# One attention kernel: the cross value sums of a half on eight blocks of TensorE at once, in one slot

## The reference, cut to what matters

```
q, k, v   = heads(xn @ Wq + bq), heads(xn @ Wk + bk), heads(xn @ Wv + bv)
y         = softmax(mask(q k^T) * scale) @ v                  # self
qc,kc,vc  = heads(xn @ Wcq + bcq), heads(ctx @ Wck + bck), heads(ctx @ Wcv + bcv)
y         = y + softmax(qc kc^T * scale) @ vc                 # cross: 64 keys
x         = x + tanh(g_xattn) * (y @ Wp + bp)
x         = x + tanh(g_ffn) * ffn(layernorm(x))
```

## Time and profile before

| | |
|---|---|
| median of three runs | 1546.71 us |
| the profiled execution | 1540.59 us, its span 1538.5 us, 2.1 us lie around it |
| TensorE (PE) busy | 1426.7 us, 93% of the span |
| VectorE (DVE), ScalarE (ACT), GpSimd (POOL) busy | 74%, 58%, 59% |
| mean granted TensorE clock | 0.989 of full speed |
| attention phase | about 21 to 1122 us: 16 batches, whole ones 67.9 us each |

### The profile page before, as it was taken

One profiled execution on the slowest core, in us unless ns is written; L12 is line 12 of the kernel. 1 busy time (PEld: TensorE's weight loads), 2 busy tenths in 40 slices (PEclk: granted clock), 3 DMA queues, 4 the chain that ended last, 5 costly groups with the idle time before them and its releaser, 6 DMA issues.

```text
span 1538.5 us, 36199 instructions
## 1 busy us (share of the span) xinstructions
PE 1426.7 (93%) x11288; PEld 948.6 (62%) x11288; DVE 1145.7 (74%) x3026; ACT 896.0 (58%) x1907; POOL 901.9 (59%) x1643
## 2 busy tenths in 40 slices
PE   4899999999999999999999999999979989898997
PEld 3556556655566566555655665665546778787675
DVE  6777887878778887878788787878644555565686
ACT  3466676666667676666667666665723555565210
POOL 4245566664756666575756657475654555665782
PEclk8899999999999999999999999999999999999999
DMA  6745454545454554645464454545555565454794
GB/s 169 198 131 138 140 151 141 172 135 165 135 160 146 157 169 120 183 133 151 134 177 144 136 180 126 159 134 172 178 152 160 169 221 170 150 153 143 230 351 165
DMA packets 184123, 250.01 MB, mean 162 GB/s; under 512 B 32024, under 2 KB 134560, under 8 KB 183936
## 3 DMA queue, kind: packets, MB, share of 16 engines
q1 hardware_dynamic: 149680, 185.60, 42.0%
q0 software_dynamic: 13008, 36.65, 6.6%
q10 hardware_dynamic: 21248, 25.46, 5.0%
HBM read 150.06 MB, written 95.97 MB: 160 GB/s over the span
## 4 chain that ended last, share of the span: by engine, by line
PE 63%; DVE 18%; ACT 11%; issue 5%; DMA 2%; POOL 1%; SPq 0%; DVEq 0%; ACTq 0%; POOLq 0%
PE vector_bank L2025 8%; PE pv_self L1529 8%; DVE nmax L1288 7%; PE scalar_bank L1465 7%; PE vector_bank L1502 5%; PE vector_bank L1575 4%; PE vector_bank L1439 3%; PE vector_bank L1499 3%; ACT q L857 3%; PE scalar_bank L1452 2%; PE scalar_bank L1455 2%; PE scalar_bank L1453 2%; ACT parts L866 2%; PE scalar_bank L2012 2%; ACT parts L873 2%
## 5 line engine op out<-in xcount | busy, mean ns | idle before, releaser
L1288 DVE TENSOR_REDUCE nmax<-vector_bank 128x1 f32<-128x384 f32 (+4 forms) x832 | 511.2, 639 | 74.4 <-PE vector_bank L1502 70.0
L929 ACT ACTIVATE pt<-scalar_bank 128x512 f32<-128x512 f32 x640 | 362.7, 605 | 175.6 <-PE scalar_bank L1465 167.1
L746 POOL TENSOR_SCALAR_AFFINE_SELECT pt<-pt 128x256 f32<-128x256 f32 (+1 forms) x640 | 222.7, 362 | 206.4 <-ACT pt L929 184.4
L1465 PE MATMUL scalar_bank<-stack 99*64 99x512 bf16 (+4 forms) x1280 | 284.2, 319 | 2.3 <-ACT pt L929 1.0
L1502 PE MATMUL vector_bank<-stack 96*128 96x128 bf16 (+3 forms) x1024 | 244.0, 301 | 0.0
L1854 POOL DMA_INDIRECT rows<-pt x143 | 139.1, 973 | 117.3 <-DVE pt L1983 63.2
L1499 PE MATMUL vector_bank<-tri,ident_b 128*128 128x128 bf16 (+2 forms) x704 | 175.3, 249 | 21.5 <-DMA stack<-qk_scratch 10.5
L1529 PE MATMUL pv_self<-pt,vst 128*32 128x512 f32 (+3 forms) x2048 | 161.1, 438 | 0.1
L705 POOL DMA_INDIRECT rows<-xn,slot x128 | 132.8, 1037 | 44.2 <-issue 26.3
L1499 PEld LDWEIGHTS vector_bank<-tri,ident_b 128*128 128x128 bf16 x704 | 67.0, 97 | 145.2 <-DVE nmax L1288 59.9
L2025 PE MATMUL vector_bank<-pt 128*128 128x128 f32 x1144 | 151.2, 275 | 0.1
(11 more groups left out here) (320 smaller groups left out, 2858.9 us busy)
## 6 DMA issues: line engine op xcount, KB each, us to landing
qk_scratch<-parts SPq DMA_DIRECT2D x31, 1200.0 KB, 4.5
stack<-qk_scratch SPq DMA_DIRECT2D x120, 192.0 KB, 3.0
pt<-rows SPq DMA_DIRECT2D x143, 132.0 KB
stack<-qk_scratch SPq DMA_DIRECT2D x248, 72.0 KB, 2.5
stack<-qk_scratch SPq DMA_DIRECT2D x124, 128.0 KB, 3.0
stack<-qk_scratch SPq DMA_DIRECT2D x240, 36.0 KB, 2.1
pt<-rows SPq DMA_DIRECT2D x8, 1024.0 KB, 8.7
stack<-rows SPq DMA_DIRECT2D x8, 1024.0 KB, 11.5
```

The source lines that it names most:

```text
L746: pool.affine_select(out=v, in_=v, compare_op=ALU.is_ge, fill=0.0, base=0, pattern=pat, channel_multiplier=-1).then_inc(masked, 1)
L929: act.activation(dst, bank(kind, b, ("st", c, k))[:, :], ACT.Exp, scale=SCALE).then_inc(scalar_drained, 1)
L1288: dve.tensor_reduce(dst, src, axis=AX, op=ALU.max, negate=True).then_inc(vector_drained, 1)
L1465: return pe.matmul(out, stack[c][0:rows, head, key0:key0 + nk], stack[c][0:rows, head, q0:q0 + nq], start=True, stop=True, **kw)
```

## The change

- Cross sums: all eight heads of a half in one place, slot 14, once the exponentials of X0 and X1 of the second group are done. Each head is a block of its own: 64 rows (its 64 keys), 32 columns, 512 moving columns. The four even heads (rows 0 to 63) write `pv_cross`, the four odd heads (rows 64 to 127) write `pv_self`. `vcst` loses its zero blocks.
- ScalarE copies both behind the exponential of slot 15, and s(c, 0) behind that of slot 22.
- The first self sums, which now wait for both of these copies, go from slots 16 and 20 to 17 and 21.
- The transposes of x go to slots (0, 19), (0, 23), (1, 18) and (1, 21); `yT`, `wp`, the statistics, `mT` and `xT` go to later slots.
- `recip` has a buffer for each sum, `yc` is one buffer in which x of the even and the odd heads interleave, and `normalise` of x waits for GpSimd's last addition from it.

```diff
-PREV_UNITS = {(0, 1): ("yT", 0), (0, 2): ("yT", 1), (0, 4): ("wp", 0), (0, 5): ("wp", 1), (0, 6): ("wp", 2), (0, 7): ("wp", 3),
+PREV_UNITS = {(0, 3): ("yT", 0), (0, 4): ("yT", 1), (0, 6): ("wp", 0), (0, 7): ("wp", 1), (0, 8): ("wp", 2), (0, 9): ("wp", 3),
-ROUTE_STEPS = {(0, 5): ("stats", 0), ..., (0, 10): "aggregate", (0, 14): "normalise", (0, 23): "max", ...
+ROUTE_STEPS = {(0, 7): ("stats", 0), ..., (0, 11): "aggregate", (0, 15): "normalise", (0, 23): "max", ...
-CUR_UNITS = {(1, 6): ("tU", 0, 1, "x"), (1, 11): ("tU", 0, 1, "s"),
-             (0, 2): ("mT", 0, 1), (0, 16): ("mT", 1, 0), (1, 2): ("mT", 1, 1)}
-NEXT_UNITS = {..., (1, 13): ("xT", 0), (1, 15): ("xT", 1), (1, 16): ("mT", 0, 0)}
+CUR_UNITS = {(1, 11): ("tU", 0, 1, "s"), (0, 19): ("tU", 0, 0, "x"), (0, 23): ("tU", 0, 1, "x"),
+             (1, 18): ("tU", 1, 0, "x"), (1, 21): ("tU", 1, 1, "x"),
+             (0, 5): ("mT", 0, 1), (0, 21): ("mT", 1, 0), (1, 4): ("mT", 1, 1)}
+NEXT_UNITS = {..., (1, 14): ("xT", 0), (1, 16): ("xT", 1), (1, 20): ("mT", 0, 0)}
...
-    PV = Events(of_current([(w, c, g) for c in range(KC) for g in range(2) for w in ("x", "s")]), LB, credit=8)
+    PV = Events(of_current([(w, c, g) for c in range(KC) for w in ("x", "s") for g in range(2)]), LB, credit=8)
...
-                act.activation(usum[w, g][:, :], (pv_cross if w == "x" else pv_self)[:, :], ACT.Copy).then_inc(pv_drained, 1)
+                act.activation(usum[w, g][:, :], (pv_cross if (w, g) == ("x", 0) else pv_self)[:, :], ACT.Copy).then_inc(pv_drained, 1)
...
-                        if c == 1 and k == 3:
-                            unnormalised(kind, b, "x", 0, 1)
                         if c == 1 and k == 8:
                             unnormalised(kind, b, "s", 0, 1)
-                        if k == 18:
-                            unnormalised(kind, b, "x", c, 0)
+                        if k == 15:
+                            for i in range(2):
+                                unnormalised(kind, b, "x", c, i)
+                        if k == 22:
+                            unnormalised(kind, b, "s", c, 0)
                     if cur:
-                        unnormalised(kind, b, "s", c, 0)
                         if c == 1:
-                            unnormalised(kind, b, "x", 1, 1)
                             unnormalised(kind, b, "s", 1, 1)
...
-                    dve.wait_ge(y_added, YADD.upto(kind, b, (c, g)) - 2)
+                    dve.wait_ge(y_added, YADD.upto(kind, b, (c, 0)) - 1)
...
-            def pv_cross_products(kind, b, c, g):
-                pe.wait_ge(pv_drained, PV.upto(kind, b, ("x", c, g)) - 2)
-                pe.wait_ge(scalar_drained, SU.upto(kind, b, ("st", c, len(GROUP) * g + 1)))
-                for jp in range(2):
-                    last = pe.matmul(pv_cross[64 * jp:64 * jp + 64, :], vcst[:, c and 1 + b % 2, 2 * g + jp, :], ct[g][:, jp, :],
-                                     start=True, stop=True)
-                last.then_inc(pv_filled, 1)
+            def pv_cross_products(kind, b, c):
+
+                pe.wait_ge(pv_drained, PV.upto(kind, b, ("x", c, 0)) - 1)
+                pe.wait_ge(scalar_drained, SU.upto(kind, b, ("st", c, len(GROUP) + 1)))
+                for j in range(HU // 2):
+                    for i, ps in enumerate((pv_cross, pv_self)):
+                        rows = slice(i * TC, (i + 1) * TC)
+                        last = pe.matmul(ps[32 * j:32 * j + 32, :], vcst[rows, c and 1 + b % 2, j, :], ct[j // 2][rows, j % 2, :],
+                                         start=True, stop=True)
+                        if j == HU // 2 - 1:
+                            last.then_inc(pv_filled, 1)
 
             def pv_self_products(kind, b, c, g, kt):
                 if kt == 0:
-                    pe.wait_ge(pv_drained, PV.upto(kind, b, ("s", c, g)) - 2)
+                    pe.wait_ge(pv_drained, PV.upto(kind, b, ("s", c, g)) - 1)
...
-                    if k > 0:
-                        pv_cross_products(kind, b, c, 0)
-                    elif c == 1:
-                        pv_cross_products(kind, b, 0, 1)
                 elif start > 1:
                     score_unit(kind, b, c, k)
-                if k in (16, 20):
-                    for kt in KT_ORDER[(k - 16) // 2:(k - 12) // 2]:
+                if k == len(GROUP) + 2:
+                    pv_cross_products(kind, b, c)
+                if k in (17, 21):
+                    for kt in KT_ORDER[(k - 17) // 2:(k - 13) // 2]:
                         pv_self_products(kind, b, c, 0, kt)
...
-                    transpose_sums(kind, b, c, 0, "x")
                     if c == 1:
-                        pv_cross_products(kind, b, 1, 1)
                         for kt in KT_ORDER:
                             pv_self_products(kind, b, 1, 1, kt)
```

More of the change, by code:

```diff
@@ L147, in attention_phase @@
     BESIDE = [spread(5), spread(6)]
-    FIRST_UNITS = {(1, 0): [("sm", 0, u) for u in range(SM_PRE, NSM // 2)] + [("v", 0), ("v", 1), ("vc",)], (1, 13): [("xT", 0)], (1, 15): [("xT", 1)],
+    FIRST_UNITS = {(1, 0): [("sm", 0, u) for u in range(SM_PRE, NSM // 2)] + [("v", 0), ("v", 1), ("vc",)], (1, 14): [("xT", 0)], (1, 16): [("xT", 1)],
                    (1, 1): [("sm", 0, u) for u in range(NSM // 2, NSM // 2 + 1)] + [("mT", 0, 0)],
@@ L218, in attention_phase @@
                   LB, credit=4)
+    NORM = Events(lambda kind: ([("s", 1, 1)] if PARTS[kind][0] else []) +
+                  ([("x", 0, 0), ("x", 0, 1), ("s", 0, 0), ("s", 0, 1), ("x", 1, 0), ("x", 1, 1), ("s", 1, 0)]
+                   if PARTS[kind][1] else []), LB)
     SPLIT = Events(of_next([0, 1]), LB)
@@ L285, in attention_phase @@
         usum = {(w, g): usum_all[:, 2 * g + i, :] for i, w in enumerate(("x", "s")) for g in range(2)}
-        recip = {w: sb(f"recip_{w}", [P, QT, HEAD_GROUP]) for w in ("x", "s")}
+        recip = {(w, g): sb(f"recip_{w}{g}", [P, QT, HEAD_GROUP]) for w in ("x", "s") for g in range(2)}
         y = sb("y", [P, QT, H, D])
-        yc = [sb(f"yc{g}", [P, QT, HEAD_GROUP, D]) for g in range(2)]
+        yc = sb("yc", [P, QT, HU, D])
         yT = sb("yT", [P, KC, T])
@@ L711, in split_max @@
                 n = MSPLIT.upto(kind, b, (c, g))
-                pool.wait_ge(vector_drained, VD.start(kind, b) - (0 if kind == "first" else 2) if (c, g) == (0, 1) else
+                pool.wait_ge(vector_drained, VD.start(kind, b) - (0 if kind == "first" else 1) if (c, g) == (0, 1) else
                              VD.upto(kind, b, ("sm", c, LAST_SM[g])))
@@ L752, in add_cross @@
                 dst = y[:, :, h:h + HEAD_GROUP, :]
-                pool.tensor_tensor(dst, dst, yc[g][:, :, :, :], ALU.add).then_inc(y_added, 1)
+                pool.tensor_tensor(dst, dst, yc[:, :, HEAD_GROUP * g:HEAD_GROUP * (g + 1), :], ALU.add).then_inc(y_added, 1)
             def low_parts(kind, b, c):
@@ L880, in unnormalised @@
                     act.wait_ge(vector_filled, VU.start(kind, b))
-                elif PARTS[kind][0]:
+                elif w == "s" and PARTS[kind][0]:
                     act.wait_ge(vector_filled, VU.upto(kind, b, ("tU", 1, 1, w)))
+                else:
+                    act.wait_ge(vector_filled, VU.start(kind, b))
                 act.wait_ge(pv_filled, PV.upto(kind, b, (w, c, g)))
-                act.activation(usum[w, g][:, :], (pv_cross if w == "x" else pv_self)[:, :], ACT.Copy).then_inc(pv_drained, 1)
+                act.activation(usum[w, g][:, :], (pv_cross if (w, g) == ("x", 0) else pv_self)[:, :], ACT.Copy).then_inc(pv_drained, 1)
             def turned_rows(kind, b, name):
@@ L1092, in cross_values @@
                 twin = 1 + (LN.upto(kind, b, 0) - 1) % 2
-                for half_, col in ((0, 0), (1, 32)):
+                for half_ in range(2):
                     rows = slice(half_ * TC, (half_ + 1) * TC)
                     last = dve.tensor_tensor(
-                        vcst[rows, 0:twin + 1:twin, :, col:col + D],
+                        vcst[rows, 0:twin + 1:twin, :, 0:D],
                         ps[rows, 0:C].rearrange("p (s a i d) -> p s a i d", s=KC, i=2, d=D)[:, :, :, half_, :],
@@ L1320, in body @@
                 if prev:
-                    for w in ("x", "s"):
-                        normalise(kind, b, 1, 1, w)
+                    normalise(kind, b, 1, 1, "s")
                 if kind == "pro":
@@ L1344, in body @@
                     if cur:
-                        for w in ("x", "s"):
-                            normalise(kind, b, c, 0, w)
+                        normalise(kind, b, c, 0, "s")
             over_batches(dve, body)
@@ L1436, in transpose_sums @@
                 ps = claim_v(kind, b, ("tU", c, g, w))
-                pe.wait_ge(pv_drained, PV.upto(kind, b, (w, c, g)) if (c, g) != (1, 1) else PV.start(kind, b) - (w == "x"))
+                pe.wait_ge(pv_drained, PV.upto(kind, b, (w, c, g)) if (w, c, g) != ("s", 1, 1) else PV.start(kind, b))
                 for t in range(QT):
@@ L1666, in body @@
```

(3 more changed lines are left out.)

34 lines of the change are left out of this document (16 added, 18 removed).

## The result

| | before | after |
|---|---|---|
| median on one chip | 1545.3 us | 1588.06 us (1587.5 to 1590.12) |
| ratio | | 1.0306, 95% interval 1.0266 to 1.0346 |
| the profiled execution, its span | 1540.59, 1538.5 us | 1588.61, 1586.9 us |
| thirteen batches, one batch | 884.7, 68.05 us | 918.6, 70.66 us |

A forecast was written before the change was run, and what follows sets the result against it. TensorE (PE) was taken as the bound, VectorE close behind. Per batch -1.40 work, +2.56 waits and -0.1 given back make +1.06 us; over 15 batches 15.9 us, so 1562.6 us from a median of 1546.7, range 1527 to 1585.

The forecast's parts named there:

- PE's work: Attention phase: two groups of eight blocks (2.10) replace cross sums (3.89), plus shape prices; -1.40 us a batch.
- the change of shape: Score unit just ahead of the self sums takes 0.31 us instead of 0.22: +0.09, counted in half 1.
- The rival of serial row halves: Row halves don't run together: each group takes 0.86 us more, 26 us in all, 1588 us; chance 0.12.
- The three waits: New PE waits for ScalarE in slot 17, slot 14 and at the end of half 1: together +2.56 us a batch.
- Slot 17: Self sums wait until ScalarE has copied both banks: 0.73 us, in both halves +1.46.
- Slot 14: The eight blocks wait for X1's exponential: +0.26 us in half 0, nothing in half 1.
- End of half 1: Self sums of (1, 1) wait for ScalarE's copy of s(1, 0), behind slot 22's exponential: +0.84 us.
- What the waits give back: Half 0, slots 17 to 23: VectorE catches up, so about half of PE's 0.9 us waits go: -0.5.
- Half 1: Waits grow by about 0.2 us at B0 in slot 3 and about 0.2 for VectorE in slot 13.
- Moves that cost nothing: Later slots for `yT`, `wp` and `mT`, and `yc` as one buffer, were to cost nothing.
- the -0.1: Net of what waits give back in half 0 and the longer waits in half 1: -0.1 us a batch.
- The rival that VectorE's waits cover the new ones: PE's 2.56 us only replace waits for VectorE, so only less work counts: -21 us, 1526; chance 0.25.

The follow-up runs named there:

- early copies: Changed kernel with ScalarE's copies of x behind the exponential of slot 14, not 15, and of s(c, 0) behind slot 21, not 22: 1549.88 us, ratio 1.0044.
- old slots: Changed kernel with `yT`, `wp`, the statistics, normalise and `mT` of (0, 1) back in their earlier slots: 1581.1 us, ratio 1.0237.
- the kernel before with the same slots: Kernel before with only `yT`, `wp`, statistics, normalise and `mT` of (0, 1) in the changed kernel's later slots: 1549.35 us, ratio 1.004.

## Why the prediction was wrong

The direction and the main mechanism (new waits for ScalarE's copies) were right, the size was not: 2.84 us a batch in place of 1.06. One term came out right for a wrong reason. By its steps:

- **PE's work, forecast -1.40.** Right. Two groups at 1.02 (forecast 1.05) replace 3.89, X costs 0.10 in three places and the change of shape 0.09 (670.41 to 670.72, 0.31 in place of 0.22): -3.89 + 2.04 + 0.30 + 0.09 = -1.46. By the 4 ns of the Trainium skill, "TensorE: Matmul & The Clock Gate", Part 3, a group would have been 0.98, an estimate; the six further blocks cost 0.06 here, 0.005 each in each of two passes. The rival of serial row halves fell, although its 1588 is the time that was measured: that agreement is chance. A total doesn't tell which rival is right.
- **The three waits, forecast +2.56.** Right in place and nearly in size. Slot 17: 0.85 in half 0 (1.16 less 0.22 and the 0.09 that before pays too) and 0.91 in half 1, forecast 0.73 each. Slot 14: 0.31 (0.62 less 0.22 and 0.09), forecast 0.26. End of half 1: 0.88, forecast 0.84. Together 2.95; the early copies gave 2.50 of it back, the slot 14 wait stayed. ScalarE's side was right: in slot 17 its second copy ends 1.98 after B0's start, forecast 2.00. What I had wrong there is PE's way, as B0 and its maximum unit take 0.44 (636.87 to 637.31) and not 0.52, and the 0.06 from the copy's end (638.85) to the first self product.
- **What the waits give back, forecast -0.5 in half 0.** Right in size by luck: the maximum units of slots 12 to 23 hold TensorE for 3.20 us a batch in place of 3.76. But with early copies, where the wait of slot 17 is gone, they hold it for 3.20 as well, so it isn't that wait that lets VectorE catch up. Which of the other moves does it no run shows.
- **Half 1, forecast +0.2 and +0.2.** Too small. Its slots 0 to 11 should have become shorter by 1.34 and did so by 0.59: +0.75. Ahead of the self sums of slot 3 the loss is 0.2, as forecast; another 0.55 lie behind them, in waits for VectorE for which the sum had nothing (below). In slots 12 to 23 maximum units and the router's ranks hold TensorE 0.56 longer, forecast 0.2; that the cross sums no longer let VectorE catch up there is argued, not shown. The boundary gives 0.17 back. Together about +1.1 in place of +0.4.
- **Moves that cost nothing.** Wrong by +0.75, in half 0's slots 0 to 11. I argued that `yT` and `wp` only change places with the scores; old slots gave 0.72 back, so they don't. The later slots alone account for 0.24 of it (12.44 in place of 12.20, in the kernel before too). The other 0.51 come from one reduction of VectorE in slot 8 that starts late (last section): in the three of after's thirteen whole batches where it is on time the stretch is 12.44, in the ten others 12.93 to 12.97. Had the moved steps been left alone, the change would have been at 1.0237.

2.95 - 1.46 - 0.56 + 1.14 + 0.75 = 2.82, against 2.84 between the cuts.

So the term that failed is the -0.1 in which I put all secondary effects and the zero for the moves; together they are +1.3. That is 1.4 of the 1.8 us by which the sum fell short; the three waits are the other 0.4. Both came from the same habit: I took what PE waits for today as what it can win, and looked at no engine two steps away. In half 1 TensorE reached its waits earlier and just waited longer. These rows of half 1's slots 1 and 2 after show 0.76 and 0.49 us from a maximum unit's second product to the next score, in place of 0.22, the first for ScalarE's emptying of a projection (timeline of PE). That is 0.81 of waiting, where before the unit `mT` in slot 2 waited for VectorE instead, with 0.83 in the same place (635.61 to 636.44) and so 0.61 of waiting: the +0.2 of the forecast.

```profile
654.89 0.38 PE L1502 MATMUL vector_bank<-stack 96*128 96x512 bf16 x1
655.65 0.39 PE L1465 MATMUL scalar_bank<-stack 99*128 99x512 bf16 x1 [0.38 <-ACT q L859]
...
655.93 0.38 PE L1502 MATMUL vector_bank<-stack 96*128 96x512 bf16 x1
656.42 0.39 PE L1465 MATMUL scalar_bank<-stack 99*128 99x384 bf16 x2
```

Most of the other 0.55 stands in slot 9, where the second unit of values (L1403) starts 0.71 us after the maximum unit's last part began, in place of 0.26 (medians of nine batches); another 0.17 stands in slot 6. The timeline of PE after, and the waits of PE after and before, name VectorE:

```profile
663.61 0.39 PE L1502 MATMUL vector_bank<-stack 96*128 96x128 bf16 x4
664.33 0.50 PE L1403 MATMUL vector_bank<-w_v,xnT 128*128 128x256 f32 x2 [0.34 <-DVE nmax L1291]
```
```profile
PE vector_bank L1403 <- DVE nmax L1291: 4.7, 15, 0.3
```
```profile
PE vector_bank L1403 <- DVE nmax L1288: 0.2, 1, 0.2
```

In the same stretch VectorE was busy for 13.80 of 14.54 us, where it had been for 13.77 of 15.13 (busy times, half 1's slots 0 to 11, after and before):

```profile
653.78:668.32 14.54, 13.54 (x123) 8.23 (x122) 13.80 (x51) 9.91 (x21) 7.82 (x13) 1.00 0.68 216
```
```profile
633.15:648.28 15.13, 14.49 (x132) 9.04 (x132) 13.77 (x53) 10.34 (x22) 7.84 (x13) 1.00 0.66 220
```

**What stays open.** What holds VectorE back in slots 6 and 9 of half 1 isn't settled. Its own work is a part: the one normalisation left out ahead of slot 9 gave 0.18 back there, which is all that the stretch gained in that run. The stall beside GpSimd, 0.58 us longer than before, may be another; the runs that shortened it moved seven steps with it and became longer. No run takes ScalarE's work away in slots 1 to 3. Nor is it known why the reduction of slot 8 is late in the changed kernel and never in the kernel before with the same slots.

The rival that VectorE's waits cover the new ones fell: taking the waits out gave nearly their full length back, also one by one.

## What to carry to other kernels

A product that shares its result bank with another has to wait for the engine that empties the bank, and that wait is set by the place of the copy in the emptying engine's order, not by that engine's load: here ScalarE idled 1.28 us ahead of an exponential, 0.58 of them with the sums to be copied lying ready, and one slot earlier in its order gave 2.50 of 2.84 us back. An engine that is busy for 59% of the time can be next in line, through a chain in program order (GpSimd: from one batch's last mask to the deviations that VectorE needs, 25.1 us): before counting on a gain, follow such chains over the batch boundary, and fill their waiting gaps with work from ahead of the critical step. Work taken out of a stretch pays only up to the next engine's arrival; price each stretch between fixed points for itself. And a term that comes out right has to be tested like one that doesn't: the -0.5 came out right, and the reason given for it was wrong.

## What the runs showed of the hardware

- Eight blocks of 64 rows by 32 columns, fp32, 512 columns each, that write two banks, take 1.02 us from their start to the next instruction; two blocks of 128 rows by 64 columns took 0.96.
- Two kinds of VectorE instruction that meet GpSimd's subtraction don't end before it. The product of the probabilities takes 0.50 us when it starts 0.42 before the subtraction's end, and 1.08 when it starts 1.00 before: it ends 0.08 after it in all fourteen batches in which they meet, both times. In the last two batches, where no subtraction runs beside it, it takes 0.21 to 0.23. One of VectorE's normalisations took 2.69 in place of 0.40 in the same way (3.66 for four). The Trainium skill, "SBUF — State Buffer", section "Who interferes with whom", says that VectorE shares a pair of ports with GpSimd, that `tensor_tensor` with both inputs in SBUF reads its second input through it and `tensor_scalar` can use the pair in its faster modes, and that in these modes whoever comes second is blocked for the whole instruction. The trace agrees in that neither ends ahead of the subtraction; which mode the normalisation ran in it doesn't show. Reductions weren't held up: those of the maximum units, which read PSUM, ran at 0.68 beside the subtraction, and one of 64 columns in SBUF at 0.21.
- In half 0's slot 8 of after, the reduction of a maximum unit whose last product was followed at 629.72 by two products of `wp` (four records) began only at 630.84, with VectorE idle for 0.62 us and, by the profile, released by those later products. This recurs in ten of thirteen whole batches; in the other three the same reduction starts 0.45 us after that last product began, in place of 1.15 or more, so the program doesn't make it wait for `wp`. In the kernel before with the same slots it is on time in all thirteen. What holds the signal back isn't known (timelines of PE and VectorE after, then of the kernel before with the new slots):

```profile
629.48 0.40 PE L1495 MATMUL vector_bank<-stack 96*128 96x64 bf16 x8
629.72 1.11 PE L1579 MATMUL vector_bank<-w_p,yT 128*128 128x256 f32 x4
```
```profile
630.84 0.69 DVE L1291 TENSOR_REDUCE nmax<-vector_bank 128x8 f32<-128x512 f32 x1 [0.62 <-PE vector_bank L1579]
```
```profile
612.30 1.11 PE L1575 MATMUL vector_bank<-w_p,yT 128*128 128x256 f32 x4
```
```profile
612.72 0.68 DVE L1288 TENSOR_REDUCE nmax<-vector_bank 128x8 f32<-128x512 f32 x1
```
